# A graph layer with its edges grouped by node: every node's own loop leaves the edge list, 16 gathered chunks a tile in place of 17

## The reference, cut to what matters

```python
src = jnp.concatenate([_s, _d, _loop])
dst = jnp.concatenate([_d, _s, _loop])
_o = jnp.argsort(dst, stable=True)
...
deg_out = jnp.clip(jax.ops.segment_sum(ones, src, num_segments=n), 1.0)
deg_in = jnp.clip(jax.ops.segment_sum(ones, dst, num_segments=n), 1.0)
h = feats * jax.lax.rsqrt(deg_out)[:, None]
m = jax.ops.segment_sum(h[src], dst, num_segments=n) * jax.lax.rsqrt(deg_in)[:, None]
gc = m @ W_gc + b_gc
x = gc + (feats @ W_res + b_res)
core = _moe_ff(x, Wg, bg, w1, b1, w2, b2)
y = x + core
```

## Time and profile before

| what | us |
|---|---|
| median of three runs | 3358.59 |
| lowest and highest run | 3357.26, 3359.37 |
| span of the profiled execution | 3782.8 |

### The profile page before, as it was taken

How to read it: one execution, slowest core, us unless ns; L and a number is a source line. 1 busy time by engine, 2 the same in 40 slices (tenths; PEclk the granted TensorE clock), 3 DMA queues, 4 the chain that set the end, 5 groups by cost and what they waited for, 6 DMA issues and landing times. The chain is left out here.

```text
span 3782.8 us, 61265 instructions
## 1 busy us (share of the span) xinstructions
PE 2867.3 (76%) x15295; PEld 2136.6 (56%) x15296; DVE 2006.0 (53%) x7025; ACT 1197.5 (32%) x2890; POOL 2109.8 (56%) x2156
## 2 busy tenths in 40 slices
PE   3245778787777877777777777778699999999950
PEld 3234445555545545555554555555588989888840
DVE  5369444444544444454444444444555555555598
ACT  3368112222222222222212222212244444444428
POOL 5722666666666666666666666665355555555500
PEclk7557888998998888989889888989899999999985
DMA  7622534444444434444344444434444454444387
GB/s 245 188 68 89 175 114 137 117 141 119 142 144 119 136 117 137 148 117 138 118 138 121 146 137 119 137 109 126 142 139 138 149 161 136 148 136 151 99 312 233
DMA packets 309520, 537.64 MB, mean 142 GB/s; under 512 B 47197, under 2 KB 220381, under 8 KB 307698
## 3 DMA queue, kind: packets, MB, share of 16 engines
q0 software_dynamic: 102160, 273.85, 24.8%
q1 hardware_dynamic: 206766, 259.99, 20.8%
q10 hardware_dynamic: 436, 1.85, 0.1%
HBM read 418.03 MB, written 121.75 MB: 143 GB/s over the span
## 5 line engine op out<-in xcount | busy, mean ns | idle before, releaser
L1427 POOL DMA_INDIRECT work<-h_table,src_cols x1529 | 1456.6, 953 | 785.1 <-issue 419.1
L1820 PE MATMUL ps<-work 128*128 128x257 f32 x3322 | 1056.8, 400 | 36.9 <-issue 35.0
L1820 PEld LDWEIGHTS ps<-work 128*128 128x128 f32 x3322 | 621.1, 198 | 290.7 <-issue 114.4
L1691 PE MATMUL ps<-none_w,none 128*128 128x512 bf16 x1369 | 534.2, 390 | 14.1 <-issue 13.6
L2091 PEld LDWEIGHTS ps<-xst,work 128*128 128x128 f32 x3648 | 443.4, 192 | 28.9 <-issue 17.9
L2091 PE MATMUL ps<-xst,work 128*128 128x128 f32 x3648 | 447.4, 276 | 11.6 <-issue 11.6
L1966 POOL DMA_INDIRECT picked<-ys,places x228 | 249.2, 1093 | 357.5 <-DVE ys L2036 334.8
L2098 PE MATMUL ps<-work,hid 128*128 128x256 f32 x1824 | 436.6, 382 | 0.3
L1722 PE MATMUL ps<-w_conv,turned 128*128 128x320 f32 x392 | 173.7, 579 | 268.5 <-ACT turned L1380 181.1
L1947 ACT ACTIVATE hid<-ps,b_cols 128x128 f32<-128x128 f32 x912 | 304.1, 367 | 186.2 <-PE ps L2091 119.2
L2098 PEld LDWEIGHTS ps<-work,hid 128*128 128x128 f32 x1824 | 329.0, 190 | 46.3 <-ACT hid L1947 10.5
(11 more groups left out here) (309 smaller groups left out, 4244.3 us busy)
## 6 DMA issues: line engine op xcount, KB each, us to landing
work<-in_L_gnn_w_dram SPq DMA_DIRECT2D x128, 512.0 KB
picked<-work SPq DMA_DIRECT2D x14, 1792.0 KB
work<-h_table,src_cols POOLq DMA_INDIRECT x1529
pk<-picked SPq DMA_DIRECT2D x13, 1792.0 KB
x_ahead<-work SPq DMA_DIRECT2D x105, 128.0 KB
work<-x_ahead SPq DMA_DIRECT2D x105, 128.0 KB
acc<-m_base SPq DMA_DIRECT2D x14, 903.0 KB
x_beta<-xr_x SPq DMA_DIRECT2D x98, 128.0 KB
```

The costliest lines, as they stand in the source:

```text
L1427: pool.indirect_dma_start(out=got[:, c % RING, 0:D], out_offset=None, in_=h_table[:, :], in_offset=bass.IndirectOffsetOnAxis(ap=src_cols[: ...
L1691: nc.tensor.matmul(ps[:, 7, :], none[:, :], none_w[:, :], start=False, stop=False)
L1820: mm = nc.tensor.matmul(ps_flat[:, bank(t, k, w[0])], hot[:, (2 * t + (k >= HALF)) % HOTS, k % HALF if k >= HALF else k, :], got[:, c % RI ...
```

## The change

The own loops are taken out on the chip. What is left is OE = 200000 edges in 1563 chunks, PER = 16 to a tile. The first block now loads the lists as strips of 14 overlapping rows of 144 edges, and also tests that each node's last edge, and it alone at a rise of the destination, is its loop. In `columns_and_degrees` DVE packs destination and source into one word, and squeezes the loops out of each row by four conditional moves (of 1, 2, 4 and 8 places); POOL scatters the 14 rows of every lane to `other_edges` in DRAM, SP reads them back as rows, and DVE unpacks them. The 27 early chunks have a small copy of this in the first block. The histogram has 98 groups. In the aggregation `acc` starts from each node's own row of `h_table` in place of zeros, `m_base` is gone, the in-degree is that of the bank plus one and is taken ahead of the eviction, and three of PE's tile steps stand one chunk earlier, since there is one chunk less.

```diff
-    PER = E // N
+    PER = OE // N
...
+                        for j in range(2):
+                            pool.wait_ge(early_step, EARLY_STEPS)
+                            if j > 0:
+                                pool.wait_ge(early_moved, 16)
+                            pool.indirect_dma_start(out=early_edges[:, :], out_offset=bass.IndirectOffsetOnAxis(ap=early_at[:, j:j + 1], axis=1),
+                                                    in_=early_s[:, j, 0:P], in_offset=None).then_inc(early_moved, 16)
...
+                if not general:
+                    sp.wait_ge(strip_step, 1)
+                    sp.wait_ge(rows_moved, 16 * STRIP_ROWS)
+                    full = (RJ - 1) * P
+                    back = other_edges.rearrange("a e -> (a e)")
+                    sp.dma_start(rows_s[:, 0:RJ - 1, :], back[0:full * P].rearrange("(j p e) -> p j e", p=P, e=P)).then_inc(rows_back, 16)
...
+                def place_rows(k):
+                    pool.wait_ge(rows_packed, k + 1)
+                    if k > 0:
+                        pool.wait_ge(rows_moved, 16 * HALF_ROWS)
+                    for j in range(k, STRIP_ROWS, 2):
+                        pool.indirect_dma_start(out=other_edges[:, :], out_offset=bass.IndirectOffsetOnAxis(ap=strip_at[:, j:j + 1], axis=1),
+                                                in_=packed[:, j, 0:P], in_offset=None).then_inc(rows_moved, 16)
+
+                if not general:
+                    early(0, EARLY_FIRST)
+                    place_rows(0)
+                    early(EARLY_FIRST, EARLY_THEN)
+                    place_rows(1)
+                    early(EARLY_THEN, READY)
...
+                    nc.vector.tensor_tensor(behind_first, from_d, from_d[:, :, 0:1].broadcast_to([P, HALF_ROWS, WINDOW]), ALU.subtract).then_inc(strip_step, 1)
...
+                    nc.vector.scalar_tensor_tensor(both, behind_first, float(1 << 14), from_d, ALU.mult, ALU.add).then_inc(strip_step, 1)
...
+                    nc.vector.scalar_tensor_tensor(rows, both, 14, from_s, ALU.logical_shift_left, ALU.bitwise_or).then_inc(strip_step, 1)
+                    for b in range(SHIFTS):
...
+                        nc.vector.tensor_scalar(moves[:, k, :, :], rows, 28 + b, 1, ALU.arith_shift_right, ALU.bitwise_and).then_inc(strip_step, 1)
...
+                        moved = nc.vector.copy_predicated(rows[:, :, 0:WINDOW - (1 << b)], moves[:, k, :, 1 << b:WINDOW], rows[:, :, 1 << b:WINDOW])
...
+                    pack_rows(0)
+                    pack_rows(1)
+                    dve.wait_ge(rows_back, 48)
+                    nc.vector.tensor_scalar(rows_d[:, :, :], rows_s[:, :, :], 14, (1 << 14) - 1, ALU.arith_shift_right, ALU.bitwise_and).then_inc(strip_step, 1)
+                    nc.vector.tensor_scalar(rows_s[:, :, :], rows_s[:, :, :], (1 << 14) - 1, None, ALU.bitwise_and).then_inc(strip_step, 1)
...
-        PRODUCT_AT, RANKS_AT, TURN_AT, LIST_AT = 3, 13, 15, 16
+        PRODUCT_AT, RANKS_AT, TURN_AT, LIST_AT = 3, 12, 14, 15
...
-                    sp.dma_start(acc3[:, q * SET:(q + 1) * SET, :],
-                                 by_lane(m_base)[:, bass.ds(unusual * (SET * (q + 1)), SET), :]).then_inc(base_in[q % 2], 16)
+                    sp.dma_start(acc3[:, q * SET:(q + 1) * SET, 0:D],
+                                 h_table.rearrange("(t p) d -> p t d", p=P)[:, bass.ds(unusual * NT + q * SET, SET), :]).then_inc(base_in[q % 2], 16)
...
-                    nc.vector.tensor_tensor(acc3[:, t, 0:MW], acc3[:, t, 0:MW], ps[:, t % BANKS, 0:MW], ALU.add).then_inc(evicted, 1)
+                    nc.vector.tensor_tensor(acc3[:, t, 0:D], acc3[:, t, 0:D], ps[:, t % BANKS, 0:D], ALU.add).then_inc(evicted, 1)
...
-                    dve.wait_ge(evicted, t + 1)
-                    nc.vector.tensor_scalar(deg[:, t % 2:t % 2 + 1], acc3[:, t, D:MW], 1.0, None, ALU.max).then_inc(deg_set, 1)
+                    dve.wait_ge(tile_done, t + 1)
+                    nc.vector.tensor_scalar(deg[:, t % 2:t % 2 + 1], ps[:, t % BANKS, D:MW], degree0[:, t:t + 1], 1.0, ALU.add, ALU.max).then_inc(deg_set, 1)
...
+                        degree(slot - 1)
                         evict(slot - 1)
-                        degree(slot - 1)
```

More of the change, by code:

```diff
@@ L42 @@
 CENTRED = 3
+STRIP_ROWS = 14
+WINDOW = 144
 LN_EPS = 1e-5
@@ L192, in _ @@
-                        sp.wait_ge(rows_in, 96)
+                        for early, edges in ((early_d, dst), (early_s, src)):
+                            sp.dma_start(early[:, :, :], bass.AP(edges.tensor, edges.offset, [[2 * P, EARLY_LANES], [P, 2], [1, WINDOW]])).then_inc(early_in, 16)
+                        load_strips(sp, strip_s, src, src_in)
+                        sp.wait_ge(early_moved, 32)
+                        sp.dma_start(rows_e[:, :], early_edges[0:READY, :]).then_inc(early_in, 16)
@@ new lines, in _ @@
+                        dve.wait_ge(paced, 7)
+                        for n in range(2):
+                            nc.vector.scalar_tensor_tensor(pace[:, n, :], tile_f[:, 1 - n, :], float(PER), row_at[:, :], ALU.mult, ALU.add).then_inc(paced, 1)
+                        dve.wait_ge(viol_set, 3)
+                        nc.vector.scalar_tensor_tensor(unlike, wrong, 1.0, rise, ALU.mult, ALU.mult, accum_out=vsum[:, :]).then_inc(viol_set, 1)
+                        dve.wait_ge(paced, 9)
+                        dve.wait_ge(pads_set, 4)
@@ new lines, in _ @@
+                        for part_of in ((slice(0, WHOLE + 1), slice(0, REST_ROWS)), (slice(0, WHOLE), slice(REST_ROWS, STRIP_ROWS))):
+                            nc.vector.tensor_scalar(ahead[part_of], pace[part_of[0], 0, part_of[1]], float(EARLY - 1), None, ALU.is_gt).then_inc(paced, 1)
+                            nc.vector.tensor_scalar(behind[part_of], pace[part_of[0], 1, part_of[1]], float(-LATE - PER), None, ALU.is_lt).then_inc(paced, 1)
+                        dve.wait_ge(paced, 13)
+                        nc.vector.tensor_tensor(ahead[:, :], ahead[:, :], behind[:, :], ALU.add).then_inc(paced, 1)
@@ L220, in _ @@
[L220 to L238, removed]
-                        nc.vector.tensor_tensor(vmax[:, :], vmax[:, :], vpace[:, :], ALU.max).then_inc(vmax_set, 1)
                         dve.wait_ge(vall_set, 1)
@@ L547, in columns_and_degrees, with windows @@
             f_rows = f_lanes[0:NT, :]
+            HALF_ROWS = STRIP_ROWS // 2
+            behind_first, both = (acc[:, n * HALF_ROWS * WINDOW:(n + 1) * HALF_ROWS * WINDOW].bitcast(I32).rearrange("p (j e) -> p j e", e=WINDOW)
+                                  for n in range(2))
+            moves = ps[:, 0:4, :].rearrange("p b n -> p (b n)").bitcast(I32)[:, 0:2 * HALF_ROWS * WINDOW].rearrange("p (k j e) -> p k j e", k=2, e=WINDOW)
+            def windows(strip, k):
+                return bass.AP(strip.tensor, strip.offset + k * P, [strip.ap[0], [2 * P, HALF_ROWS], [1, WINDOW]])
             stage = dstf.rearrange("p j e -> p (j e)")[:, 0:STAGED * D].rearrange("p (s d) -> p s d", d=D)
@@ L626, in columns_and_degrees @@
         QS = [0, 9, 27, 51, 75, NT]
-        h_out = [sem2(f"h_out{q}") for q in range(len(QS) - 1)]
+        h_out = sem2("h_out")
         TB = ceil_div(RJ, 4)
@@ L773, in _ @@
                 dve.wait_ge(counted, 1)
-                inverse_root(nc, dve, step, v, deg, root, newton, f_out, ps[:, 6, 0:NT], rooted)
+                inverse_root(nc, dve, step, v, deg, root, newton, f_out, ps[:, 6, 0:NT], rooted, not general)
                 dve.wait_ge(v, n[0])
@@ L858, in _ @@
                 if general:
[L859 to L861 removed]
+                    dve.wait_ge(h_out, 16 * (len(QS) - 1))
+                    nc.vector.memset(acc3[:, :, :], 0.0)
             @block.scalar
@@ L1009, in aggregate_any @@
         kept = sem2("any_kept")
-        paced = sem2("any_paced")
-        OVER = 17
-        SHARE = ceil_div(1 << OVER, PER)
-        assert all((c * SHARE) >> OVER == c // PER for c in range(CH))
         TURNS = STEPS // NB
```

286 lines of the change are left out of this document (200 added, 86 removed).

## The result

| what | us |
|---|---|
| before, median (four runs) | 3358.98 (3357.26 to 3359.61) |
| changed, median (four runs) | 3278.47 (3277.43 to 3281.05) |
| ratio, 95% interval | 0.9766 (0.9752 to 0.978) |
| span of the changed kernel's profiled execution | 3275.6 |

The changed kernel is 80.5 us faster; 3285 was forecast. This time the profiled span lies beside the times, so its trace can be read as it stands. The kernel before was therefore profiled once more (first experiment), and the comparison by stage uses that trace, whose span is 3356.9.

The account below looks back on a forecast made before the run. POOL's gather issue was taken to pace the aggregation, with the first profile's stalls mostly its own. Fewer gathers -123.0 and a longer front +49.5 sum to -73.5: 3285 us, own range 3255 to 3310 (3250 to 3340 with rivals, chance 0.8).

Parts of the forecast that it names:

- Forecast -123.0: Aggregation: 98 fewer gathers at POOL's spacing of 1.255 us each; bounds -63.7 to -143.3.
- The rival in which PE paces: Aggregation: PE paces without profile too, a chunk is worth 0.65 us; 3344 us, chance 0.12.
- the slower one that rests on it: Aggregation: PE paces and each tile waits for its mean at the earlier transposes; 3388 us, chance 0.05.
- the 20 to 25 us that stayed unexplained: Part of the median before that POOL's pace did not explain; counted in favour of PE pacing.
- The first cast was to come 60.0 us later: Front: checks, packing, scatters, read back and unpacking delay the first cast, from 21.57 to 81.6 us.
- The +8 for a late POOL: Front: early gathers and seven scatters end after the second packing, at 60.4 not 52.4 us; range 0 to 16.
- the terms named on the low side: Low end 3255: packing at 15 (-11), scatters free (-8), checks (-2), read back (-2).
- The rival in which POOL is held off by the whole packing: Front: fifteen POOL transfers start only after packing, ending at 72, 12 us later than taken; 3297 us, chance 0.10.
- 6.1 behind the unstalled histogram: Front before: last `x_ahead` write ends at 224.0 us, histogram at 217.9; after the change 7.8 behind, costed 0.
- the -10.5 us for six groups less: Front: histogram six groups shorter at 1.757 us each, taken whole off the front, making it +49.5.
- there is no cover left: Front: any further delay of the loads of x goes to the front's end; stores and factor gathers queue behind.
- The rival of loads and staged rows last: Front: loads of x or staged rows become last; loads half as long again, 22 us more; 3307 us, chance 0.09.

Follow-up runs that it names:

- first experiment: Kernel before, unchanged, profiled once more; 3358.62 us, span 3356.9 us.
- experiments 1 to 3: Kernel before: 1 profiled again, 3358.62 us; 2 with 95 gathers left out, PE's work kept, 3235.19; 3 with 95 PE products left out, gathers kept, 3342.55.
- experiments 3 and 8: 3: kernel before with 95 PE products left out, 3342.55 us; 8: changed kernel with the transposes at chunk 11 in place of 14, 3279.12 us.
- experiment 6: Changed kernel with 77 staged chunks in place of 91; 3283.39 us.
- experiment 7: Changed kernel with the histogram's 104 groups of before in place of 98; 3282.74 us.
- experiment 9: Changed kernel with every mask of the packing written three times, 16 more DVE instructions; 3298.36 us.

## Why the prediction was right, and where its steps were not

**The bound and the gain.** That POOL's issue paces the aggregation without profile too was inferred from sums; experiments 1 to 3 show it. Forecast -123.0, measured -123.3. The rival in which PE paces, and the slower one that rests on it, fall with experiments 3 and 8. The rest of that inference was less good: I took the front before for 266.5 us and what lies behind the aggregation for 1152.8, and they are 292.5 and 1142.1. So the 20 to 25 us that stayed unexplained stood in the front, and no pace of PE was needed for them.

**The head.** The first cast was to come 60.0 us later; it came 56.3 later (21.85 to 78.13). Step by step: the checks end at 24.05 (21.9 forecast). The gap to the first packing instruction is 7.9 us, not the 4.1 carried over from the earlier trace rows. The packing takes 27.7 (26.4); a conditional move takes 1.24 to 1.31 us, so 1.2 was the right price. The +8 for a late POOL did not occur. The seven scatters take 8.6 (9.7), landing and read back 7.5 (9.2). Two steps too small by 3.8 and 2.2 stood against one too large by 7.7; the others are off by less than 2 each. So that 60.0 came near 56.3 is in part luck. In the range, the terms named on the low side add up to -23, which gives 3262 and not 3255.

**POOL under the packing.** I took half of what the earlier trace rows show. The scatters and gathers there took this:

```profile
46.14 1.68 POOL L809 DMA_INDIRECT other_edges<-acc,strip_at  x1 [4.43 <-DVE acc L861]
...
53.18 0.95 POOL L809 DMA_INDIRECT other_edges<-acc,strip_at  x1 [0.30 <-issue]
54.44 0.96 POOL L809 DMA_INDIRECT other_edges<-acc,strip_at  x1 [0.30 <-issue]
55.70 0.99 POOL L801 DMA_INDIRECT work<-in_x_dram,src_early  x1 [0.31 <-issue]
```

Only the first scatter took longer, by 0.7 us; beside the packing's other instructions of 1.21 us there was no hold-up. The rival in which POOL is held off by the whole packing is wrong here. The Trainium skill, page "SBUF — State Buffer", section "SBUF: two separate sides", says that POOL cannot write the descriptors of its transfers while DVE runs an instruction in a two-port mode, and that a DVE instruction with two inputs from SBUF contends only with POOL work that reads SBUF. The 14.75 us of experiment 6 agree with the first in kind, but no row shows in which mode DVE ran, and POOL was held there through a row of instructions and not one.

**Behind the first cast.** This is the step that failed: the last staged write "6.1 behind the unstalled histogram", and with it the -10.5 us for six groups less. The staged writes stood 30 us behind the histogram before (251.44 against 221.65) and 26 after, so the histogram does not end the front, as experiment 7 shows: a change of 10.5 us there is worth about 3. I had read the 149.5 us of the earlier trace rows from a trace in which DVE stood still for part of that time, and there 78 of POOL's 105 staged gathers took 0.95 us. In the trace of experiment 1 only 22 do; 67 take 1.45, beside the histogram's masks, so that POOL issues one every 1.75 us for most of the stage, and the 105 writes take 171.7.

What really made 56.3 into 40.7 is cover that the old order had: idle time of SP's queue, which the later start now fills. Before, SP began its loads of x at 27.97 though the first cast was at 21.85, 6.1 us later, because it waited for POOL's constants; now the gap is 1.1: -5.0. The loads of x take 42.3 before and 40.8 now: -1.6. Before, SP had ended them at 70.30 and waited until 79.75 for POOL's first staged row; now POOL is there first and waits 16 us for SP: -9.4.

```profile
126.86 0.94 POOL L832 DMA_INDIRECT work<-in_x_dram,src_cols  x1 [16.25 <-DMA x_ahead<-work]
```

The staged writes take 0.7 more, the stores to the first gather 0.4 less. 56.3 - 5.0 - 1.6 - 9.4 + 0.7 - 0.4 = 40.6. The sum of 16 us from these covers stood by chance near the 10.5 of a histogram that is not on the path. That after the change "there is no cover left" behind SP's queue was right, and experiment 9 shows it one to one.

**The rival of loads and staged rows last** named the right place and the wrong time: they do end the front, but they did so before as well, so they add nothing to the delay that they pass on.

## What to carry to other kernels

A profile whose span stands far from the times should be taken again before a slack is read from it: here the sum of the aggregation survived (1919 us against 1922.3), that of the front (266.5 against 292.5) and the slack behind the histogram (6.1 against 30) did not. Where one queue carries the work of several stages in order (here SP: read back, loads, staged writes, stores), a step put ahead of it cost its whole length (experiment 9), less the time that the queue had been idle before; what it was waiting for before tells how much is free. Two orders, loads early and stores off that queue, gave back 17 of the 41 us that the change costs in the front.

## What the runs showed of the hardware that was not expected

POOL took different times to issue an indirect transfer beside different work of DVE, in three grades. Beside int32 work at 1.21 us for 1008 elements it took 0.95 to 0.99, as it does beside an idle DVE, but for the first of the early gathers (1.19) and of the scatters (1.68). Beside the histogram's bf16 masks it is mostly 1.45, and 0.95 from the moment that they end. Timelines of the changed kernel at the end of the histogram, POOL and DVE:

```profile
264.27 1.46 POOL L832 DMA_INDIRECT work<-in_x_dram,src_cols  x1 [0.30 <-issue]
266.03 0.95 POOL L832 DMA_INDIRECT work<-in_x_dram,src_cols  x1 [0.30 <-issue]
```
```profile
263.93 0.98 DVE L930 TENSOR_TENSOR work<-hi_b,values 128x1568 bf16<-128x1568 bf16 x1
264.82 0.82 DVE L932 TENSOR_TENSOR work<-lo_b,values 128x1280 bf16<-128x1280 bf16 x1
```

Beside an unbroken row of 65 fp32 scalings one issue took 14.75 us (experiment 6). In the changed kernel the same scalings run beside gathers of 0.95 us, and there it is DVE that is slower: 20.29 us for the 65, against 17.38 in experiment 6. No run took the masks or the scalings away alone, so that they are the cause is read from the times at which the durations change, not shown by an edit.
